# The 16 rows of each stack block are laid seven partitions apart instead of next to each other

## The chip, the cores and the metric

One core of a Trainium2 chip. The metric is the device time of one execution in microseconds (us), the median over several runs. A change counts as faster or slower from 2% on.

## What is computed

Four attention layers on one image of 16 x 16 places with 192 channels (12 heads of 16). Each layer is added to its input after a group norm: `x = x + layer(gn(x))`.

```
layer 0, 3: q,k,v = x@W + b;  a = (q*s)@k.T + rel_h[..., :, None] + rel_w[..., None, :]   # rel = q . table
            out = softmax(a) @ v @ proj + b
layer 1:    layernorm; q,k turned by position; a = q@k.T + bias_head[same or other token]; softmax; @v @wo;
            + residual; layernorm; gelu(x@w1 + b1)@w2 + b2; + residual
layer 2:    keys and values extended by 16 registers; a = q@k_cat.T * s, masked to a 7 x 7 neighbourhood;
            softmax; @v_cat @ out_w.T + b
```

All values are float32.

## The kernel before

Each layer runs in the same stages: group norm, projections to queries, keys and values, filling of two stacks, then for 12 heads the row maxima, scores, exponentials and value products, and the output projection.

**The stacks.** `QS` (two of them, used in turn by layer: layers 0 and 2 the first, 1 and 3 the second) and `KS` hold for each head 128 rows (partitions) over which one matmul contracts. A value is kept as a high and a low part in a short float format, so that the product of a query and a key is three terms, each a block of 16 rows (the head dimension): high times high, low times high, high times low. The blocks lie at partitions 0, 16 and 32 of both stacks. Rows 48 to 63 are zero. Rows 64 to 127 hold four more blocks of 16: the relative position terms of layers 0 and 3 (row high, column high, row low, column low), the token bias of layer 1 or the mask of layer 2; on the key side they hold `hot`, the one-hot rows and columns of each place.

**How they are filled.** SP, the sync engine, issues transfers from SBUF to SBUF. The `move` helper (L307 to L310) waits for the source's signal and issues one transfer to one block; its source is `QH`, `QL`, `KH`, `KL` (96 partitions of 2 KB, two heads each), `QHL` (rows 0 to 63 high, 64 to 127 low parts, in layers 0 and 3), or `RH`, `RL` (row terms in the lower, column terms in the upper 64 partitions). A block is 16 partitions of 12 heads of 256 places, 192 KB. The key stack has 304 places in a head, so its rows are written in pieces of 1 KB. GpSimd issues at the start `hot`, three blocks of zeros and later the mask; it computes layer 1's bias rows itself (L394), from columns that VectorE makes in `bias_cols` (L590 to L599). The registers' keys go into the edges of `KS` by six small transfers of GpSimd (L405).

**Order on TensorE.** After the projections (and `relative`, L849, in layers 0 and 3), `keep_warm(..., DMA_WARM[l])` (L1055) issues 3, 22, 17 or 21 matmuls on `WARM` whose results nobody reads. Then TensorE waits for the stacks (L1056 to L1059). After that `for_maxima` (L870) computes each head's scores for their row maxima, which VectorE reduces (`maximum`, L731, instruction at L738), `turn_early` and `turn_maxima` (L883, L891; instruction at L896) bring the negated maxima into rows, and `scores` (L911) computes the scores again, transposed, with the maxima subtracted by a second matmul. The first `EARLY` = 2 heads are turned by themselves with matmuls that contract over two rows only. Scores are followed by `values` (L926, instruction at L940) after ScalarE's exponential.

In layer 0, VectorE also works off `registers`, `bias_cols` and `reg_selector` (L785 to L787) before its first maximum. After layer 0's last stack transfer SP issues the weights of all later layers (L332, L333).

Of the kernel before, what the change touches and what calls it, by code (L numbers as in the profile page):

```python
# [15 lines left out]
T = SIDE * SIDE  # L49
# [3 lines left out]
HD = 16  # L53
NH = C // HD
HPC = CC // HD
P = 128
# [6 lines left out]
NREG = 16  # L63
# [3 lines left out]
KEY0 = NREG  # L67
REG1 = KEY0 + T
# [8 lines left out]
MASKED = -2.0 ** 100  # L77
LAYERS = 4
REL_LAYERS = (0, 3)

TERMS = ((0, 0), (0, 1), (1, 2))
Q2 = NG * P


VEC = {name: 2 * n for n, name in enumerate(
# [3 lines left out]
SCALED = ("w0", "w2", "w1", "wp", "w3")  # L91

def build(nc, a, out):
    with ExitStack() as ctx:
# [3 lines left out]
        def key_column(l):  # L100

            return Q2 if l in REL_LAYERS else C

        def ps(name, shape):
            return ctx.enter_context(nc.psum_tensor(name, shape, F32))


# [11 lines left out]
        QH = sb("QH", [CC, NC, T], F32R)  # L119
        QL = sb("QL", [CC, NC, T], F32R)  # L120
        KH = sb("KH", [CC, NC, T], F32R)
        KL = sb("KL", [CC, NC, T], F32R)

        QD = sb("QD", [P, NG, T])
        QHL = sb("QHL", [P, NG, T], F32R)
# [6 lines left out]
        RH = sb("RH", [P, NG, T], F32R)  # L132
        RL = sb("RL", [P, NG, T], F32R)
        QS = [sb(f"QS{i}", [P, NH, T], F32R) for i in range(2)]
        KS = sb("KS", [P, NH, KW], F32R)
# [29 lines left out]
        HOT = sb("HOT", [P, T])  # L165
# [5 lines left out]
        ABS = sb("ABS", [P, 3, NH])  # L171
        REGT = sb("REGT", [CC, NC, P])
        KRF = sb("KRF", [CC, NC, NREG])
        KRH = sb("KRH", [CC, NC, NREG], F32R)
        KRL = sb("KRL", [CC, NC, NREG], F32R)
# [6 lines left out]


        RINGS = [[ps(f"RING{r}{i}", [P, 512]) for i in range(2)] for r in range(2)]
# [4 lines left out]
        def hidden(m):  # L189

            return PR[:, m // 2, m % 2 * T:(m % 2 + 1) * T]


# [48 lines left out]
        def slot(*use):  # L242
# [24 lines left out]
                    "qh": {0: NG, 1: 1, 2: NC, 3: NG}, "ql": {0: 1, 1: 1, 2: NC, 3: 1},  # L267
                    "q stack": {0: 2 * 16, 1: 3 * 16, 2: 3 * 16, 3: 2 * 16}}
        signals |= {"kf": {1: 1}}
# [11 lines left out]
        def sem(name):  # L281
            return sems[name]
# [12 lines left out]
        block = ctx.enter_context(nc.Block())  # L295


        @block.sync
        def _(sync):
            def load(wanted):  # L300
                for name, tile, src in wanted:
                    dst = tile[:, :, :] if len(tile.shape) == 3 else tile[:, :]
                    sync.dma_start(dst, a[src]).then_inc(sem(f"{name} loaded"), 16)

            load(loads)
            for l in range(LAYERS):
                def move(signal, stack, src, done, count=None):  # L307

                    sync.wait_ge(*upto(signal, l, count or signals[signal][l]))
                    sync.dma_start(stack.bitcast(F32), src.bitcast(F32)).then_inc(sem(done), 16)  # L310

                queries = QS[l % 2]
                if l in REL_LAYERS:
                    move("qh", queries[32:48, :, :], QHL[0:64, :, :], "q stack")
                else:
                    for row in (0, 32):
                        move("qh", queries[row:row + HD, :, :], QH[:, :, :], "q stack")
                    move("ql", queries[16:32, :, :], QL[:, :, :], "q stack")
                for row in (0, 16):
                    move("kh", KS[row:row + HD, :, KEY0:REG1], KH[:, :, :], "k stack")  # L320
                if l in REL_LAYERS:
                    move("ql", queries[0:32, :, :], QHL[:, :, :], "q stack")
                move("kl", KS[32:48, :, KEY0:REG1], KL[:, :, :], "k stack")
                if l in REL_LAYERS:

                    for w in range(2):
                        for name, row, src in (("rel h", 64, RH), ("rel l", 96, RL)):
                            move(name, queries[row + HD * w:row + HD * w + HD, :, :], src[64 * w:64 * w + 64, :, :],
                                 "rel stack", 2 * w + 2)
                if l == 0:  # L330

                    sync.wait_ge(*upto("rel stack", 0, 64))  # L332
                    load(later_loads)  # L333

            sync.wait_ge(*upto("x", 3, NC))
            sync.dma_start(out, X[:, :, :]).then_inc(sem("stored"), 16)
            sync.wait_ge(sem("stored"), 16)


        @block.gpsimd  # L340
        def _(pool):
            g = nc.gpsimd
# [9 lines left out]
            for col in (slice(0, KEY0), slice(REG1, KW)):  # L352
                g.memset(KS[:, :, col].bitcast(F32), 0.0).then_inc(sem("keys zero"), 1)
            pool.wait_ge(sem("keys zero"), 2)

            pool.dma_start(KS[64:128, :, KEY0:REG1], a["hot"][64:128, None, :].to_broadcast([64, NH, T]))\
                .then_inc(sem("hot rows"), 16)
            for stack in (KS[48:64, :, KEY0:REG1], QS[0][48:64, :, :], QS[1][48:64, :, :]):
                pool.dma_start(stack, a["zeros"]).then_inc(sem("zero rows"), 16)


# [20 lines left out]
            for l in range(LAYERS):  # L382
                if l == 2:

                    pool.wait_ge(*upto("scores", 0, NH))
                    pool.dma_start(QS[0][64:128, :, :], a["mask"][64:128, None, :].to_broadcast([64, NH, T]))\
                        .then_inc(sem("mask rows"), 16)
                if l == 0:


                    pool.wait_ge(sem("ab cols"), 1)
                    loaded(pool, "hot")
                    for h in range(NH):
                        g.tensor_scalar(QS[1][64:128, h, :], HOT[64:128, :], ABS[64:128, 2, h:h + 1],  # L394
                                        ABS[64:128, 1, h:h + 1], ALU.mult, ALU.add).then_inc(sem("ab rows"), 1)
                        pool.wait_ge(sem("ab rows"), h + 1)
                    scale_keys("w1", WQKV[1])
                    scale_keys("wp", WP)
                    scale_keys("w3", WQKV[3], Q2)
                if l == 1:  # L400

                    pool.wait_ge(sem("kr parts"), 2)
                    for col in (0, REG1):
                        for row, src in ((0, KRH), (16, KRH), (32, KRL)):
                            pool.dma_start(KS[row:row + HD, :, col:col + NREG], src[:, :, :])\  # L405
                                .then_inc(sem("kr stack"), 16)


        @block.scalar
        def _(act):  # L410
# [110 lines left out]


            act.preload_act_table_set("natural_log_exp_and_others")
# [36 lines left out]


        @block.vector
        def _(dve):
# [26 lines left out]
            def bias_cols():  # L590

                loaded(dve, "abt", "pcol")
                r = slice(64, 128)
                link(V.tensor_copy(ABH[r], ABT[r]))
                link(V.tensor_tensor(ABL[r], ABT[r], ABH[r].bitcast(F32), ALU.subtract))
                link(V.tensor_scalar(ABS[r, 0:2], ABH[r].bitcast(F32), PCOL[r, 0:1], None, ALU.mult))
                link(V.scalar_tensor_tensor(out=ABS[r, 0:2], in0=ABL[r], scalar=PCOL[r, 1:2], in1=ABS[r, 0:2],
                                            op0=ALU.mult, op1=ALU.add))
                V.tensor_tensor(ABS[r, 2], ABS[r, 0], ABS[r, 1], ALU.subtract).then_inc(sem("ab cols"), 1)  # L599
# [176 lines left out]
            for l in range(LAYERS):  # L776
# [23 lines left out]
                else:  # L800
# [12 lines left out]
                    for i in range(NC):  # L813
                        V.tensor_tensor(X[:, i, :], X[:, i, :], FL[:, i, :], ALU.add).then_inc(sem("x"), 1)


        @block.tensor
        def _(pe):
# [179 lines left out]
            for l in range(LAYERS):  # L998
# [22 lines left out]
                else:  # L1021
                    last = project(lambda m: chunk_psum("q", l, m), WQKV[l], 0, XN, *ready, "q psum" if l == 2 else None)
# [22 lines left out]
                if l == 0:  # L1045
                    registers()
                    pe.wait_ge(sem("hot rows"), 16)
                    pe.wait_ge(sem("zero rows"), 48)
                    pe.wait_ge(sem("backgrounds"), 4)
                if l == 1:  # L1050
                    pe.wait_ge(sem("ab rows"), NH)
                if l == 2:
                    pe.wait_ge(sem("mask rows"), 16)
                    pe.wait_ge(sem("kr stack"), 6 * 16)
# [65 lines left out]


def layouts(inp):
# [3 lines left out]


    order = np.arange(C).reshape(HPC, NC, HD).transpose(1, 2, 0).reshape(C)


# [48 lines left out]
    hot = np.zeros((P, T), f32)  # L1179
    hot[64:80] = hot[96:112] = row == k  # L1180
    hot[80:96] = hot[112:128] = col == k
    first = np.clip(np.arange(SIDE) - 3, 0, SIDE - 7)
    mask = np.zeros((P, T), f32)
    mask[64:80] = np.where((k >= first[row]) & (k < first[row] + 7), 0, MASKED)
    mask[80:96] = np.where((k >= first[col]) & (k < first[col] + 7), 0, MASKED)
    angles = HD // 4
# [6 lines left out]
    pcol = np.zeros((P, 3), f32)  # L1193
    pcol[64:80, 0] = 1
    pcol[96:112, 1] = 1
    pcol[:, 2] = np.arange(P) % 32 < NREG
# [3 lines left out]
    abt = np.zeros((P, 2, NH), f32)  # L1200
    abt[64:128] = L["L1_conv_attn_biases"].T
    regt = np.zeros((CC, NC, GH, 32), f32)
# [14 lines left out]


# [12 lines left out]
```

## Time and profile before

| | |
|---|---|
| Time, median of 3 runs | 290.22 us (287.61 to 291.16) |
| Span of the profiled execution | 287.2 us (the profile gives no other time of it) |
| TensorE busy | 241.8 us (84%), 1255 matmuls; weight loads 149.7 us |
| VectorE busy | 106.3 us (37%) |
| ScalarE busy | 78.7 us (27%) |
| GpSimd busy | 25.3 us (9%) |
| Mean granted TensorE clock | 0.869 of full |
| DMA | 10574 packets, 15.06 MB; 12.63 MB on the queue of SP, 2.24 MB on that of GpSimd |

Busy shares are means over the whole span, in which TensorE's work includes matmuls on `WARM`. A name such as `QS<-QH` is "tile written <- tile read"; buffer numbers are left out. SPq is SP's queue of DMA issues; PE is TensorE, DVE VectorE, ACT ScalarE, POOL GpSimd.

### The profile page before, as it was taken

The page shows a single profiled execution, that of the slowest core. Times are in us where ns is not written, and L with a number is a line of the kernel's source. Part 1 is how long each engine was busy: PE and PEld are TensorE (multiplying, and loading weights), DVE is VectorE, ACT ScalarE, POOL GpSimd, SP SyncE. Part 2 cuts the span into 40 slices and gives each one's busy share as a digit, 9 for nine tenths or more (in the row PEclk, how much of TensorE's full clock was granted, in tenths as well). Part 3 has the DMA queues.
Part 4 walks back from the last instruction along what each step waited for, and adds up shares of the span by engine and source line. Part 5 has one row for each costly group of instructions (what it writes and reads, how often), then busy time and mean ns, then how long its engine had stood idle before and what let it go on. Part 6 is the DMA issues. An engine that isn't in the chain of part 4 may idle for free.

```text
span 287.2 us, 3244 instructions
## 1 busy us (share of the span) xinstructions
PE 241.8 (84%) x1255; PEld 149.7 (52%) x1266; DVE 106.3 (37%) x262; ACT 78.7 (27%) x156; POOL 25.3 (9%) x45
## 2 busy tenths in 40 slices
PE   7856069999899579999989874999999877499995
PEld 2754046555357256655466443665564762375552
DVE  4566034324638133424311522321125651334222
ACT  2581003432030002342252200224321470023431
POOL 7510812601000000000000000000000000000000
PEclk9975557999999955999999996589999977658999
DMA  6999959409003900000000093000000089200000
GB/s 171 236 153 133 123 139 308 69 3 110 2 1 51 113 0 0 2 0 2 0 0 0 3 124 40 0 0 2 0 0 2 27 109 118 21 0 0 0 3 27
DMA packets 10574, 15.06 MB, mean 52 GB/s; under 512 B 2912, under 2 KB 7296, under 8 KB 10528
## 3 DMA queue, kind: packets, MB, share of 16 engines
q1 hardware_dynamic: 7472, 12.63, 28.0%
q0 software_dynamic: 3088, 2.24, 6.3%
q8 instruction: 10, 0.16, 0.3%
q14 instruction: 4, 0.03, 0.0%
HBM read 8.30 MB, written 0.20 MB: 30 GB/s over the span
## 4 chain that ended last, share of the span: by engine, by line
PE 63%; DMA 15%; DVE 7%; ACT 7%; issue 5%; SPq 2%; DVEq 0%; ACTq 0%
PE PC L940 15%; DMA QS<-RL 9%; PE RING L922 8%; PE RING L879 8%; PE RING L923 6%; DMA QS<-QL 4%; PE PB L960 4%; PE RING L824 4%; PE PC L951 2%; DMA RELT<-in_relt 2%; PE PC L865 2%; PE RING L1111 2%; PE PA L1117 2%; PE PC L943 2%; PE PB L824 1%
## 5 line engine op out<-in xcount | busy, mean ns | idle before, releaser
L738 DVE TENSOR_REDUCE NM<-RING 128x2 fp32r<-128x512 f32 (+1 forms) x48 | 30.8, 658 | 73.9 <-PE RING L879 73.5
L879 PE MATMUL RING<-KS,QS 128*128 128x256 f32 (+1 forms) x96 | 28.4, 404 | 28.2 <-DMA QS<-RL 17.4
L824 PE MATMUL RING<-WARM 128*128 128x512 bf16 x195 | 50.0, 401 | 2.3 <-POOL WARM L343 1.3
L940 PE MATMUL PC<-PR,VX 128*32 128x256 f32 x192 | 47.6, 395 | 0.0
L506 ACT ACTIVATE PR<-RING 128x512 f32<-128x512 f32 x48 | 28.6, 595 | 43.0 <-PE RING L923 42.5
L879 PEld LDWEIGHTS RING<-KS,QS 128*128 128x128 f32 x96 | 20.6, 268 | 36.2 <-issue 33.5
L922 PE MATMUL RING<-QS,KS 128*128 128x256 f32 x96 | 34.3, 374 | 0.3
L824 PEld LDWEIGHTS RING<-WARM 128*128 128x128 bf16 x206 | 20.9, 104 | 25.5 <-issue 4.9
L923 PE MATMUL RING<-MT,SELM 128*128 128x256 f32 (+1 forms) x96 | 30.4, 332 | 0.0
L922 PEld LDWEIGHTS RING<-QS,KS 128*128 128x128 f32 x96 | 20.3, 212 | 16.1 <-issue 10.6
L940 PEld LDWEIGHTS PC<-PR,VX 128*32 128x32 f32 x192 | 16.5, 111 | 17.3 <-issue 3.2
L923 PEld LDWEIGHTS RING<-MT,SELM 128*128 128x128 f32 (+1 forms) x96 | 20.4, 213 | 3.3 <-issue 2.7
L494 ACT ACTIVATE MT<-PA 2x256 fp32r<-2x256 f32 x4 | 1.5, 373 | 59.7 <-PE PA L888 59.7
L746 DVE COPY U<-PC 128x256 f32<-128x256 f32 x12 | 5.1, 424 | 27.2 <-PE PC L940 17.4
L751 DVE SCALAR_TENSOR_TENSOR LD<-PC,RD 128x256 f32<-128x256 f32 x12 | 5.1, 425 | 26.4 <-ACT RD L520 26.4
L960 PE MATMUL PB<-O,WO 128*96 128x256 f32 x48 | 12.9, 392 | 0.0
L960 PEld LDWEIGHTS PB<-O,WO 128*96 128x96 f32 x48 | 7.2, 162 | 4.9 <-DVE O L755 1.7
L500 ACT ACTIVATE MT<-PA 128x256 fp32r<-128x256 f32 x12 | 4.6, 382 | 18.6 <-PE PA L896 18.6
L519 ACT ACTIVATE LD<-PC 128x256 f32<-128x256 f32 x12 | 4.6, 386 | 15.3 <-PE PC L951 15.3
L394 POOL TENSOR_SCALAR QS<-HOT,ABS 64x256 fp32r<-64x256 f32 x12 | 6.7, 560 | 14.2 <-DVE ABS L599 13.1
L951 PE MATMUL PC<-U,BSEL 128*128 128x256 f32 x24 | 7.8, 405 | 0.0
L865 PE MATMUL PC<-QC,RELB 128*64 128x48 bf16 x96 | 5.5, 228 | 2.5 <-ACT QC L479 2.5
(153 smaller groups left out, 262.8 us busy)
## 6 DMA issues: line engine op xcount, KB each, us to landing
KS<-KH SPq DMA_DIRECT2D x8, 192.0 KB, 6.8
WQKV<-in_w SPq DMA_DIRECT2D x2, 576.0 KB, 7.2
WO<-in_wo SPq DMA_DIRECT2D x4, 288.0 KB, 9.1
W<-in_ff SPq DMA_DIRECT2D x2, 576.0 KB, 7.6
WQKV<-in_w SPq DMA_DIRECT2D x2, 432.0 KB, 6.6
KS<-in_hot POOLq DMA_DIRECT2D x1, 768.0 KB, 15.4
QS<-QHL SPq DMA_DIRECT2D x2, 384.0 KB, 11.4
KS<-KL SPq DMA_DIRECT2D x4, 192.0 KB, 8.6
```

Source lines behind the costliest of these rows:

```text
L394: g.tensor_scalar(QS[1][64:128, h, :], HOT[64:128, :], ABS[64:128, 2, h:h + 1], ABS[64:128, 1, h:h + 1], ALU.mult, ALU.add).then_inc(sem(" ...
L506: A(PR[:, h % NPR, :], slot("e", l, h)[:, :], ACT.Exp).then_inc(sem("probs"), 1)
L738: V.tensor_reduce(NM[g % 2][:, :, h % GH], slot("m", l, h)[:, 0:2 * n_keys].rearrange("p (q k) -> p q k", q=2), AX.X, ALU.max, negate=True ...
L824: M(bank, WARM[:, 0:P], WARM[:, :], start=True, stop=True)
L865: ins = M(terms.rearrange("p (g c) -> p g c", g=NG), lhsT, q, start=(t == 0), stop=(t == len(TERMS) - 1))
L879: ins = M(s[:, q * n_keys:(q + 1) * n_keys], QS[l % 2][:, h, q * P:(q + 1) * P], KS[:, h, keys], start=True, stop=True)
L922: M(dst, KS[:, h, KEY0 + k * P:KEY0 + (k + 1) * P], QS[l % 2][:, h, :], start=True, stop=False)
L923: ins = M(dst, sel, mt, start=False, stop=True)
L940: ins = M(dst, VX[:, k, h, :], PR[:, h % NPR, k * T:(k + 1) * T], start=(k == 0), stop=(k == 1 and l != 2))
L943: ins = M(dst, VR[:, h, :], PG[g % 2][:, :], start=False, stop=True)
L951: M(PC[g % 2][:, T:2 * T], BSEL[:, :], U[g % 2][:, :], start=True, stop=True)\
L960: ins = M(PB[0:CC, m * T:(m + 1) * T], WO[l][:, g, m * CC:(m + 1) * CC], O[g][:, :], start=(g == 0 and m == 0), stop=(g == NG - 1), skip_g ...
```

## The change

The stacks' rows are dealt out anew. With `BLOCKS = 7` blocks and `FREE = 128 - 7*16 = 16` rows left at the bottom, block b's row k lies at partition 16 + b + 7k. All tensors made outside (`hot`, `mask`, `pcol`, `abt`) follow. What is computed stays the same; a matmul contracts over all 128 rows in any order.

```
+BLOCKS = 7
+FREE = P - BLOCKS * HD
+Q_HIGH, Q_LOW, Q_AGAIN, ROW_HIGH, COL_HIGH, ROW_LOW, COL_LOW = range(BLOCKS)
...
+        def rows_of(stack, block, first=0, last=T):
+            return stack[FREE + block:P:BLOCKS, :, first:last]
...
-                    "q stack": {0: 2 * 16, 1: 3 * 16, 2: 3 * 16, 3: 2 * 16}}
+                    "q stack": {l: 3 * 16 for l in range(LAYERS)}}
...
                 if l in REL_LAYERS:
-                    move("qh", queries[32:48, :, :], QHL[0:64, :, :], "q stack")
+                    for block in (Q_AGAIN, Q_HIGH):
+                        move("qh", rows_of(queries, block), QHL[0:64, :, :], "q stack")
                 else:
-                    for row in (0, 32):
-                        move("qh", queries[row:row + HD, :, :], QH[:, :, :], "q stack")
-                    move("ql", queries[16:32, :, :], QL[:, :, :], "q stack")
-                for row in (0, 16):
-                    move("kh", KS[row:row + HD, :, KEY0:REG1], KH[:, :, :], "k stack")
+                    if l == 1:
+                        sync.wait_ge(sem("ab rows"), NH)
+                    for block in (Q_HIGH, Q_AGAIN):
+                        move("qh", rows_of(queries, block), QH[:, :, :], "q stack")
+                    move("ql", rows_of(queries, Q_LOW), QL[:, :, :], "q stack")
+                for block in (Q_HIGH, Q_LOW):
+                    move("kh", rows_of(KS, block, KEY0, REG1), KH[:, :, :], "k stack")
                 if l in REL_LAYERS:
-                    move("ql", queries[0:32, :, :], QHL[:, :, :], "q stack")
-                move("kl", KS[32:48, :, KEY0:REG1], KL[:, :, :], "k stack")
+                    move("ql", rows_of(queries, Q_LOW), QHL[64:128, :, :], "q stack")
+                move("kl", rows_of(KS, Q_AGAIN, KEY0, REG1), KL[:, :, :], "k stack")
                 if l in REL_LAYERS:
                     for w in range(2):
-                        for name, row, src in (("rel h", 64, RH), ("rel l", 96, RL)):
-                            move(name, queries[row + HD * w:row + HD * w + HD, :, :], src[64 * w:64 * w + 64, :, :],
-                                 "rel stack", 2 * w + 2)
+                        for name, block, src in (("rel h", ROW_HIGH, RH), ("rel l", ROW_LOW, RL)):
+                            move(name, rows_of(queries, block + w), src[64 * w:64 * w + 64, :, :], "rel stack", 2 * w + 2)
...
-            pool.dma_start(KS[64:128, :, KEY0:REG1], a["hot"][64:128, None, :].to_broadcast([64, NH, T]))\
-                .then_inc(sem("hot rows"), 16)
-            for stack in (KS[48:64, :, KEY0:REG1], QS[0][48:64, :, :], QS[1][48:64, :, :]):
+            for block in (ROW_HIGH, COL_HIGH, ROW_LOW, COL_LOW):
+                pool.dma_start(rows_of(KS, block, KEY0, REG1),
+                               a["hot"][FREE + block:P:BLOCKS, None, :].to_broadcast([HD, NH, T])).then_inc(sem("hot rows"), 16)
+            for stack in (KS[0:FREE, :, KEY0:REG1], QS[0][0:FREE, :, :]):
                 pool.dma_start(stack, a["zeros"]).then_inc(sem("zero rows"), 16)
...
-                        g.tensor_scalar(QS[1][64:128, h, :], HOT[64:128, :], ABS[64:128, 2, h:h + 1],
-                                        ABS[64:128, 1, h:h + 1], ALU.mult, ALU.add).then_inc(sem("ab rows"), 1)
+                        g.tensor_scalar(QS[1][:, h, :], HOT[:, :], ABS[:, 2, h:h + 1], ABS[:, 1, h:h + 1], ALU.mult, ALU.add).then_inc(sem("ab rows"), 1)
...
-                r = slice(64, 128)
+                r = slice(0, P)
...
```

The mask of layer 2 and `hot` are each written by four transfers of one block instead of one of 64 partitions, and the registers' keys go to the same blocks. GpSimd's bias rows now fill all 128 rows of layer 1's query stack (the other blocks with zeros, since their columns are zero), and this is why SP waits for them (`ab rows`) before it writes the queries of layer 1, and why the zeros of the second query stack are no longer transferred. In layers 0 and 3 the high parts of the queries go out twice by a transfer each; before, the second copy went with the low parts in one transfer to 32 rows. The counts on which TensorE waits follow.

## Rows read from the trace of the kernel before

**Rows 1.** The page, 40 slices of 7.18 us: granted TensorE clock in tenths, and GB/s.

```profile
PEclk9975557999999955999999996589999977658999
GB/s 171 236 153 133 123 139 308 69 3 110 2 1 51 113 0 0 2 0 2 0 0 0 3 124 40 0 0 2 0 0 2 27 109 118 21 0 0 0 3 27
```

**Rows 2.** TensorE in order of time: start us, length us, work [idle before it <-releaser].

```profile
38.71 1.19 PE L879 MATMUL RING<-KS,QS 128*128 128x256 f32 x4 [12.17 <-DMA QS<-RL]
...
92.27 4.91 PE L824 MATMUL RING<-WARM 128*128 128x512 bf16 x21
102.12 1.19 PE L879 MATMUL RING<-KS,QS 128*128 128x256 f32 x4 [4.93 <-issue]
...
166.77 3.83 PE L824 MATMUL RING<-WARM 128*128 128x512 bf16 x16
176.45 1.14 PE L879 MATMUL RING<-KS,QS 128*128 128x192 f32 x4 [5.85 <-issue]
...
236.27 6.25 PE L824 MATMUL RING<-WARM 128*128 128x512 bf16 x20 [0.33 <-issue]
247.79 1.19 PE L879 MATMUL RING<-KS,QS 128*128 128x256 f32 x4 [5.26 <-DMA QS<-RL]
```

**Rows 3.** SP's queue in order of time: start us and length us of an issue.

```profile
23.96 0.60 SPq L310 DMA_DIRECT2D QS<-RL  x1
...
93.25 1.26 SPq L310 DMA_DIRECT2D KS<-KH  x2
94.55 0.62 SPq L310 DMA_DIRECT2D KS<-KL  x1
...
164.44 1.32 SPq L310 DMA_DIRECT2D QS<-QH  x2
...
167.76 0.62 SPq L310 DMA_DIRECT2D KS<-KL  x1
...
237.08 0.59 SPq L310 DMA_DIRECT2D QS<-RL  x1
```

**Rows 4.** DMA issues near 23.96, 90.00, 94.55, 167.76, 237.08 us; KB, us to landing.

```profile
QS<-RL SPq DMA_DIRECT2D x1, 192.0 KB, 14.5
...
QS<-QH SPq DMA_DIRECT2D x1, 192.0 KB, 3.9
...
KS<-KL SPq DMA_DIRECT2D x1, 192.0 KB, 7.5
...
KS<-KL SPq DMA_DIRECT2D x1, 192.0 KB, 8.6
...
QS<-RL SPq DMA_DIRECT2D x1, 192.0 KB, 10.5
```

**Rows 5.** Stretches of 2 us: TensorE busy (instructions), clock, DMA busy share, GB/s.

```profile
42.00:44.00 2.00, 2.00 (x9) 1.00 1.03 281
...
92.00:94.00 2.00, 1.95 (x10) 1.00 1.06 120
...
96.00:98.00 2.00, 1.19 (x6) 1.00 1.15 114
...
106.00:108.00 2.00, 2.00 (x6) 0.50 0.00 0
...
166.00:168.00 2.00, 2.00 (x12) 1.00 1.06 157
```

**Rows 6.** VectorE in order of time, layer 0, columns as in rows 2.

```profile
28.35 0.20 DVE L580 COPY SELR<-IDF 128x64 f32<-128x64 f32 x1
39.52 1.29 DVE L738 TENSOR_REDUCE NM<-RING 128x2 fp32r<-128x512 f32 x2 [10.97 <-PE RING L879]
```

**Rows 7.** TensorE in order of time: the second turn of maxima, layers 0, 1, 3.

```profile
49.59 0.34 PE L896 MATMUL PA<-IDR,NM 128*128 128x128 f32 x2
...
114.85 0.34 PE L896 MATMUL PA<-IDR,NM 128*128 128x128 f32 x2
...
261.07 0.34 PE L896 MATMUL PA<-IDR,NM 128*128 128x128 f32 x2
```

More of the change, by code:

```diff
@@ L385, in _ @@
                     pool.wait_ge(*upto("scores", 0, NH))
-                    pool.dma_start(QS[0][64:128, :, :], a["mask"][64:128, None, :].to_broadcast([64, NH, T]))\
-                        .then_inc(sem("mask rows"), 16)
+                    for block in (ROW_HIGH, COL_HIGH, ROW_LOW, COL_LOW):
+                        pool.dma_start(rows_of(QS[0], block), a["mask"][FREE + block:P:BLOCKS, None, :].to_broadcast([HD, NH, T]))\
+                            .then_inc(sem("mask rows"), 16)
                 if l == 0:
@@ L403, in _ @@
                     for col in (0, REG1):
-                        for row, src in ((0, KRH), (16, KRH), (32, KRL)):
-                            pool.dma_start(KS[row:row + HD, :, col:col + NREG], src[:, :, :])\
+                        for block, src in ((Q_HIGH, KRH), (Q_LOW, KRH), (Q_AGAIN, KRL)):
+                            pool.dma_start(rows_of(KS, block, col, col + NREG), src[:, :, :])\
                                 .then_inc(sem("kr stack"), 16)
@@ L1046, in _ @@
                     registers()
-                    pe.wait_ge(sem("hot rows"), 16)
-                    pe.wait_ge(sem("zero rows"), 48)
+                    pe.wait_ge(sem("hot rows"), 4 * 16)
+                    pe.wait_ge(sem("zero rows"), 2 * 16)
                     pe.wait_ge(sem("backgrounds"), 4)
@@ L1052, in _ @@
                 if l == 2:
-                    pe.wait_ge(sem("mask rows"), 16)
+                    pe.wait_ge(sem("mask rows"), 4 * 16)
                     pe.wait_ge(sem("kr stack"), 6 * 16)
@@ L1179, in layouts @@
     hot = np.zeros((P, T), f32)
-    hot[64:80] = hot[96:112] = row == k
-    hot[80:96] = hot[112:128] = col == k
+    block = [slice(FREE + b, P, BLOCKS) for b in range(BLOCKS)]
+    hot[block[ROW_HIGH]] = hot[block[ROW_LOW]] = row == k
+    hot[block[COL_HIGH]] = hot[block[COL_LOW]] = col == k
     first = np.clip(np.arange(SIDE) - 3, 0, SIDE - 7)
     mask = np.zeros((P, T), f32)
-    mask[64:80] = np.where((k >= first[row]) & (k < first[row] + 7), 0, MASKED)
-    mask[80:96] = np.where((k >= first[col]) & (k < first[col] + 7), 0, MASKED)
+    mask[block[ROW_HIGH]] = np.where((k >= first[row]) & (k < first[row] + 7), 0, MASKED)
+    mask[block[COL_HIGH]] = np.where((k >= first[col]) & (k < first[col] + 7), 0, MASKED)
     angles = HD // 4
@@ L1193, in layouts @@
     pcol = np.zeros((P, 3), f32)
-    pcol[64:80, 0] = 1
-    pcol[96:112, 1] = 1
+    pcol[block[ROW_HIGH], 0] = 1
+    pcol[block[ROW_LOW], 1] = 1
     pcol[:, 2] = np.arange(P) % 32 < NREG
@@ L1200, in layouts @@
     abt = np.zeros((P, 2, NH), f32)
-    abt[64:128] = L["L1_conv_attn_biases"].T
+    abt[:] = L["L1_conv_attn_biases"].T
     regt = np.zeros((CC, NC, GH, 32), f32)
```

## Prediction

> **What bounds the kernel now.** I read the page's slices first: four valleys in TensorE's granted clock (slices 4 to 6, 15 and 16, 25 and 26, 33 to 36, counted from 1), each in or right behind slices in which DMA moves about 110 to 150 GB/s, while one slice of weight loads moves 308 [rows 1]. These are the four layers' hand-overs: the projections are done, the stacks QS and KS are being filled, and no score can be computed. TensorE in order of time [rows 2] gives the four waits: the first `for_maxima` starts at 38.71, 102.12, 176.45 and 247.79, after 12.17, 4.93, 5.85 and 5.26 us of idle time, together 28.2; warm-up matmuls end at 97.18, 170.60 and 242.52 in layers 1 to 3 (start plus length). The view calls two of them "issue", but the transfers explain them: the last one issued before each wait [rows 3] lands so long after its issue [rows 4]: 23.96 + 14.5 = 38.5, 94.55 + 7.5 = 102.05, 167.76 + 8.6 = 176.4, 237.08 + 10.5 = 247.6. Each is within 0.25 us of TensorE's start. So the waits are transfers and nothing else.
>
> **Why these transfers are slow.** In layers 1 and 2 six transfers of 192 KB (1.18 MB) are in flight and move 114 to 120 GB/s with all DMA engines shown busy [rows 5]. The queries (runs of 2 KB, a source row) go at 120 at 92 to 94 us, the keys (runs of 1 KB, since a head of KS is wider than its 256 places) at 114 at 96 to 98; a price per packet would have made the two differ. The fastest such stretch is 166 to 168 us with 157 GB/s [rows 5]: there a write to partitions 16 to 31 (QL) is in flight beside one to 32 to 47. That speaks for a limit on the place of the destination: 16 neighbouring partitions share few ways in. Weight loads, written to 96 or 128 partitions, go at 281 GB/s on the same queue [rows 5].
>
> The Trainium skill, "SBUF — State Buffer", section "Door 1: The DMA port swizzle", has this as a rule: a partition's bits 4 to 2 and 6 choose one of 16 ports, partitions 0 to 15 reach 4 ports and measured 104 GB/s, all 128 reach 16 and measured 328. The trace's 114 and 281 agree. By that map each block of the change (16 + b + 7k) reaches 14 or 15 ports, with at most two rows on one.
>
> **The change, part by part.**
> The stack transfers keep their count of bytes, runs and source order; only their 16 destination rows spread over 106 partitions. Rate afterwards: no row shows SBUF to SBUF at a spread destination. Bounds: 157 (that fastest stretch) and 308 GB/s (loads). I take 250, nearer the loads, since the spread is like theirs, but 64 source partitions (QHL, RH, RL) may narrow the reading. A transfer's latency beside its data: the first QS<-QH of layer 1, alone in the queue, landed after 3.9 us [rows 4]; 197 thousand bytes at 115 GB/s is 1.7, leaving 2.2, of which about half lies before the data. At 250 a lone transfer would land after 2.2 + 0.8 = 3.0.
>
> Layer 1: keys are issued from 93.25 to 94.55 [rows 3]; the queries (0.59 MB from about 91.1) are gone by 93.5 at 250. Keys' data: 94.3 + 590/250 = 96.7, plus 1.1 = 97.8. The warm-up matmuls end at 97.18, so they cap the gain at 4.93; I take 102.1 − 97.8 = 4.3. At 157: data until about 98.6, landing at 99.7, gain 2.4.
> Layer 2: all six are issued within 3.3 us from 164.44. 165.5 + 1180/250 + 1.1 = 171.3, gain 5.1; cap 5.85 (cover until 170.60); at 157: 174.1, gain 2.3.
> Layer 3: the last is issued at 237.08, and at 250 GB/s little is queued before it (1.97 MB in all from 228.7 on, 7.9 us): it lands near 240.1, 2.4 us under the cover of the 20 warm-up matmuls that end at 242.52. Gain 5.26, the whole wait. At 157 the data take 12.5 us, until 241.2, plus 1.1: 242.3, just covered.
> Layer 0: to 14.4 us (2 slices of 7.18 at 171 and 236 GB/s, 2.92 MB) loads run freely. Slices 3 to 5 move 153, 133 and 123 [rows 1]: 2.94 MB. The change takes 0.2 MB of it away (zeros of the second query stack, now written by GpSimd). 2.74 MB at 250 are done at 25.4; the last issue at 23.96 lands at 27.0. At 157: 31.9 + 1.1 = 33.0. What is late next is VectorE: its work for the registers and the layer 1 bias ends at 28.55, and the first maximum started at 39.52 [rows 6]. So it can start 10.9 earlier; at 157 GB/s 5.7.
> Waits together: 10.9 + 4.3 + 5.1 + 5.3 = 25.6; at 157: 5.7 + 2.4 + 2.3 + 5.3 = 15.7; caps: 10.9 + 4.93 + 5.85 + 5.26 = 26.9.
>
> The clock. After the waits of layers 1 to 3 the granted clock lies at 0.5 (1.2 GHz) into the twelfth microsecond: at 106 to 108 it is 0.50 though TensorE is never idle there, after 1.00 up to the wait [rows 5]. From the first `for_maxima` to the turn of the second set of maxima (L896) takes 114.85 − 102.12 = 12.73 in layer 1 and 261.07 − 247.79 = 13.28 in layer 3, but 49.59 − 38.71 = 10.88 in layer 0 [rows 2, 7], where the clock was back at 1.00 from 42 to 44 [rows 5]. With a wait of 0 to 0.7 us the clock has no idle stretch to fall in, and I take layer 0's length for layers 1 and 2, gains of 1.9 each, and 13.28 − 10.88 = 2.4 for layer 3. Layer 2's stretch has register matmuls between, but its clock is low as long. Layer 0 goes the other way: it starts while the clock is down, in another phase of it; priced with layer 1's length it loses 12.73 − 10.88 = 1.9. Sum: 1.9 + 1.9 + 2.4 − 1.9 = 4.3. Bounds: 0 and 9 (a stretch never slowed, estimated at 9.5 us from layer 0's, less 3.2 us at half clock at its start and 2.7 us later, in all four layers).
>
> The Trainium skill, "TensorE: Matmul & The Clock Gate", section "HAM oscillation — how this bites in real kernels", says that waits for DMA put the clock down each time and that the next work starts cold. The rows at 106 to 108 us agree.
>
> Edits that cost nothing. One more SP issue in layers 0 and 3 (QHL's high half twice instead of 32 rows at once), 0.6 us [rows 3]: it goes out with the first signal, while SP waits for the keys' signal behind it; uncovered it would be those 0.6. GpSimd issues 6 transfers instead of 4 at the start, at about the same length 1.2 us more, before it scales w0's keys; the query projection runs meanwhile on TensorE, and without that cover it would cost up to 1.2. Four mask transfers for one go out after layer 0's scores, a whole layer before their use. The 12 `tensor_scalar` of L394 and five of `bias_cols` work on 128 partitions for 64 with the same number of elements in each, and so at equal length; layer 1 reads their result 50 us later. SP's new wait on "ab rows" is met long before layer 1; the query and key transfers are queued behind it, but their own signals come later. The later weight loads start 11 us sooner and land long before layer 1.
>
> **The sum.** 25.6 + 4.3 = 29.9; the span of 287.2 becomes 257.3. The profiled execution's span is 3.0 under the median of the three runs (290.22, from 287.61 to 291.16; the profile gives no total of its own), so 290.2 − 29.9 = 260.3; if its own time was that of the fastest run, 257.7. I predict 260.
>
> **Rivals.**
> A. The spread helps, but only to some 157 GB/s: several engines still meet on one way in, or 64 source partitions bind. Gains 15.7, and with leftover waits of 2 to 4 us half of the clock's part: 18, time 272. For it: the only mixed SBUF to SBUF stretch. Against it: its two groups of 16 were still packed.
> B. Each transfer is limited by the engines' handling, not by the destination's place. Nothing changes, one more issue: 290. For it: no transfer between SBUF tensors is seen above 157. Against it: equal rates for runs of 1 and 2 KB, and the jump to 157 with two groups.
> C. On the other side: rows that aren't neighbours are cut into more or worse distributed pieces, so that a transfer runs on half the engines' rate. Deciding point: a rate under 114 GB/s. At 57 the 1.18 MB of layers 1 and 2 take 10.3 us more each, layers 0 and 3 about as much or more: slower by over 40, 330. Against it: each row of a stack is 12 KB by itself before and after, and nothing can be merged across partitions in either.
> D. Waits go, but the clock stays down: the maxima phase with its two-row matmuls lets it fall by itself, as it did in layer 0 between 44 and 48 us even without idle time. 25.6 alone, 264.6; with layer 0 losing 2, 266. For it: that second fall.
>
> **How the numbers follow.** Forecast 0.60 (253 to 264), D 0.16, A 0.13, B 0.06, C 0.03, and 0.02 for more than forecast, down to 250. A range from 253 to 270 takes the forecast, D and a part of A, whose other part, B, C and the low end are left out: about 0.8. About 2% (5.8 us) is what a measurement of this kernel tells from no change. Faster by over 2%: forecast, D, A and the low end: 0.91; within 2%: B, 0.06; slower: C, 0.03.
>
> **What would show it.** Per step: last landings 3 to 4 us after issue instead of 7.5 to 14.5; DMA at 200 to 300 GB/s in the hand-overs; TensorE's first `for_maxima` within 1 us of its warm-up matmuls in layers 1 to 3; the first maximum of layer 0 at 28.6; clock 1.00 across the hand-overs and stretches of 10 to 11 us to L896. I would be wrong if landings stayed at 7 us or more (B), or if the stretches kept 12.7 (D).

## The result

The median fell from 289.22 us (4 runs, 287.61 to 291.16) to 259.13 us (4 runs, 256.18 to 260.93): 30.1 us or 10%. Executions of a program fall into a faster and a slower state, and the ratio of 0.8878 (95% interval 0.8817 to 0.8938), 11% less, compares fast ones alone, which for the changed kernel are those of 257.62 and 256.18 us. The profiled executions have spans of 287.2 and 255.5 us, 31.7 apart. The forecast of 260, faster, held.

The page of the changed kernel: TensorE's granted clock in tenths, and GB/s, in 40 slices, now of 6.39 us; and the two DMA queues with packets, MB and their share of 16 engines' span.

```profile
PEclk9995555999999999999999999899999997979999
GB/s 153 259 195 188 169 275 218 14 0 122 1 4 0 125 60 0 3 0 3 0 0 0 0 50 138 0 0 3 0 0 3 0 103 191 16 0 0 1 3 31
...
q1 hardware_dynamic: 7504, 12.63, 20.7%
q0 software_dynamic: 3152, 2.04, 5.1%
```

Three of the four valleys of [rows 1] have nearly closed; the first is as deep as it was. SP's queue moved the same 12.63 MB in 20.7% of a shorter span instead of 28.0%: its packets stood in the engines for less time.

TensorE in order of time, with the waits that answer to [rows 2] and the second turn of maxima (L859, L896 before) that answers to [rows 7]:

```profile
29.66 1.20 PE L842 MATMUL RING<-KS,QS 128*128 128x256 f32 x4 [5.24 <-DMA QS<-RL]
43.44 0.52 PE L859 MATMUL PA<-IDR,NM 128*128 128x128 f32 x2
...
86.35 4.91 PE L787 MATMUL RING<-WARM 128*128 128x512 bf16 x22
91.74 0.72 PE L842 MATMUL RING<-KS,QS 128*128 128x256 f32 x4 [0.48 <-issue]
100.80 0.34 PE L859 MATMUL PA<-IDR,NM 128*128 128x128 f32 x2
...
152.74 3.83 PE L787 MATMUL RING<-WARM 128*128 128x512 bf16 x17
157.43 0.66 PE L842 MATMUL RING<-KS,QS 128*128 128x192 f32 x4 [0.85 <-issue]
169.09 0.35 PE L859 MATMUL PA<-IDR,NM 128*128 128x128 f32 x2
...
214.01 5.14 PE L787 MATMUL RING<-WARM 128*128 128x512 bf16 x21
218.81 0.83 PE L842 MATMUL RING<-KS,QS 128*128 128x256 f32 x4
229.38 0.34 PE L859 MATMUL PA<-IDR,NM 128*128 128x128 f32 x2
```

The waits went from 12.17, 4.93, 5.85 and 5.26 us to 5.24, 0.48, 0.85 and none. In layer 3 `for_maxima` stands right behind the warm-up matmuls, as forecast.

The last transfers before these points, issues at 23.91, 88.62, 154.22 and 215.23 us, with KB and us to landing (answers to [rows 4]: 14.5, 7.5, 8.6, 10.5):

```profile
QS<-RL SPq DMA_DIRECT2D x1, 192.0 KB, 5.5
...
KS<-KL SPq DMA_DIRECT2D x1, 192.0 KB, 3.0
...
KS<-KL SPq DMA_DIRECT2D x1, 192.0 KB, 3.1
...
QS<-RL SPq DMA_DIRECT2D x1, 192.0 KB, 3.1
```

Stretches of 2 us, columns as in [rows 5] (TensorE busy, clock, DMA share, GB/s): layer 0 first, then the hand-overs of layers 1 and 2.

```profile
16.00:18.00 2.00, 0.83 (x26) 1.00 1.54 110
18.00:20.00 2.00, 2.00 (x53) 1.00 1.15 121
20.00:22.00 2.00, 0.96 (x8) 0.59 1.01 141
22.00:24.00 2.00, 2.00 (x7) 0.50 1.10 221
24.00:26.00 2.00, 0.41 (x1) 0.50 1.11 249
...
86.00:88.00 2.00, 2.00 (x12) 1.00 0.71 214
...
96.00:98.00 2.00, 2.00 (x12) 1.00 0.00 0
...
154.00:156.00 2.00, 2.00 (x11) 1.00 0.95 276
```

Layer 2's burst of six transfers goes at up to 276 GB/s where it went at 114 to 157, and at 96 to 98 us, two microseconds into layer 1's scores, the clock is 1.00. (A second profile of the same kernel, the "same again" of the last table, has 0.60 at 94 to 96 us and 0.54 at 96 to 98, in the same work.) But in layer 0 the rate is 110 to 141 GB/s from 16 to 22 us, as if nothing had been spread; only then does it rise.

**Where 31.7 us came from.** Each is a difference of two rows, start against start. Waits (end of the work before, or landing, to the first `for_maxima`): 38.71 − 29.66 = 9.05 in layer 0 (TensorE's own idle time fell by 6.93, since the work before it ended 2.1 us sooner, which counts for nothing while the landing comes last); in layer 1 the gain up to `for_maxima` is 102.12 − 91.74 = 10.38, of which 92.27 − 86.35 = 5.92 was there before its warm-up, so 4.46; in layer 2 likewise 19.02 − 14.03 = 4.99; in layer 3 28.98 − 22.26 = 6.72, of which 5.26 is the wait and 1.46 a faster warm-up at a higher clock. Waits together: 23.8. From first `for_maxima` to the second turn: 10.88 became 13.78 in layer 0 (−2.90), 12.73 became 9.06 in layer 1 (+3.67), 14.46 became 11.66 in layer 2 (+2.80, with the turn at 190.91 in the profile of before), 13.28 became 10.57 in layer 3 (+2.71). With the 1.46 the clock's part is 7.7. The rest is 0.2. The second profile of the changed kernel gives the clock 5.5 by the same differences: −0.01, +2.44, +1.65 and +1.45, and nothing from layer 3's warm-up.

### The profile page after: what moved, and what is told of

It is laid out like the page before. It is cut to its first block, busy times and chain, and to the rows that moved or that the text cites. A ratio compares the mean times of both kernels' runs of the same rounds, so it can differ in the third digit from the quotient of the medians.

```text
span 255.5 us, 3263 instructions
## 1 busy us (share of the span) xinstructions
PE 232.7 (91%) x1266; PEld 142.0 (56%) x1266; DVE 105.8 (41%) x262; ACT 78.6 (31%) x156; POOL 27.1 (11%) x50
## 3 DMA queue, kind: packets, MB, share of 16 engines
q1 hardware_dynamic: 7504, 12.63, 20.7%
## 4 chain that ended last, share of the span: by engine, by line
PE 73%; DVE 8%; ACT 7%; SPq 4%; DMA 4%; issue 2%; DVEq 0%; ACTq 0%
PE PC L903 17%; PE RING L787 9%; PE RING L885 9%; PE RING L886 6%; PE RING L842 6%; PE PB L923 5%; SPq L277 3%; PE PC L914 2%; DMA QS<-RL 2%; PE RING L1074 2%; PE PA L1080 2%; PE PC L806 2%; PE PC L906 2%; DMA RELT<-in_relt 2%; PE PA L806 1%
## 5 line engine op out<-in xcount | busy, mean ns | idle before, releaser
L787 PE MATMUL RING<-WARM 128*128 128x512 bf16 x206 | 51.9, 400 | 1.3 <-POOL WARM L311 1.3
L885 PE MATMUL RING<-QS,KS 128*128 128x256 f32 x96 | 32.7, 358 | 1.4 <-ACT MT L460 0.8
L842 PE MATMUL RING<-KS,QS 128*128 128x256 f32 (+1 forms) x96 | 23.5, 345 | 6.8 <-DMA QS<-RL 5.2
L886 PE MATMUL RING<-MT,SELM 128*128 128x256 f32 (+1 forms) x96 | 28.6, 315 | 0.0
L885 PEld LDWEIGHTS RING<-QS,KS 128*128 128x128 f32 x96 | 19.5, 203 | 16.4 <-issue 10.4
L903 PEld LDWEIGHTS PC<-PR,VX 128*32 128x32 f32 x192 | 16.5, 111 | 17.1 <-issue 2.9
L842 PEld LDWEIGHTS RING<-KS,QS 128*128 128x128 f32 x96 | 16.7, 223 | 14.4 <-issue 10.7
L886 PEld LDWEIGHTS RING<-MT,SELM 128*128 128x128 f32 (+1 forms) x96 | 19.5, 203 | 2.5 <-issue 0.9
L923 PE MATMUL PB<-O,WO 128*96 128x256 f32 x48 | 12.9, 392 | 0.0
L362 POOL TENSOR_SCALAR QS<-HOT,ABS 128x256 fp32r<-128x256 f32 x12 | 6.7, 554 | 13.1 <-DVE ABS L563 12.0
L396 ACT ACTIVATE GT<-GT 96x2 f32<-96x2 f32 x4 | 0.8, 203 | 22.1 <-DVE GT L585 22.1
```

The lines of the kernel that those rows point to most:

```text
L362: g.tensor_scalar(QS[1][:, h, :], HOT[:, :], ABS[:, 2, h:h + 1], ABS[:, 1, h:h + 1], ALU.mult, ALU.add).then_inc(sem("ab rows"), 1)
L787: M(bank, WARM[:, 0:P], WARM[:, :], start=True, stop=True)
L842: ins = M(s[:, q * n_keys:(q + 1) * n_keys], QS[l % 2][:, h, q * P:(q + 1) * P], KS[:, h, keys], start=True, stop=True)
L885: M(dst, KS[:, h, KEY0 + k * P:KEY0 + (k + 1) * P], QS[l % 2][:, h, :], start=True, stop=False)
L886: ins = M(dst, sel, mt, start=False, stop=True)
L903: ins = M(dst, VX[:, k, h, :], PR[:, h % NPR, k * T:(k + 1) * T], start=(k == 0), stop=(k == 1 and l != 2))
```

## The experiments

Three questions: is it the place of the destination rows and nothing else in the change; what about the place counts; and how much is the clock, in particular why layer 0 gained less of the wait than forecast and lost on its clock. The runs came in three sets, with medians of "before" of 290.7, 289.7 and 290.1 us.

**Packed: the new kernel with its rows side by side.**

```
-            return stack[FREE + block:P:BLOCKS, :, first:last]
+            return stack[block_rows(block), :, first:last]
+def block_rows(b):
+    return slice(16 * ((b + 1) % 8), 16 * ((b + 1) % 8) + 16)
```

(The tensors made outside follow, and the zero rows are a block too, in this and the next three.)

> The changed kernel with its rows put next to each other again (block b at partitions 16(b+1) to 16(b+1)+15); the doubled query copy, the split hot and mask transfers and the one zero transfer less stay. Theory (the place of the destination rows makes it all): the waits of layers 1 to 3 are back at 4 to 6 us, the last transfers land 7 to 11 us after issue, 114 to 120 GB/s; layer 0's first for_maxima near 37 (0.2 MB less). Time 284 to 291. Rival (the other edits help): waits under 3 us, time under 275.

290.92 us median, ratio to before 1.0017 (0.9974 to 1.0060). The last transfers landed 14.6, 7.5, 8.3 and 10.4 us after issue, TensorE waited 11.64, 4.99, 5.90 and 5.17 us. Everything that the layout gave is gone, and the other edits (a second copy of the high parts, four transfers in place of one, one block of zeros less) are together worth nothing measurable. The first `for_maxima` of layer 0 came at 39.3 us, where 37 was expected for the 0.2 MB less.

**Strides of 2, 4 and 8.**

```
stride 2:   return slice(32 * (b // 2) + b % 2, 32 * (b // 2) + 32, 2)
stride 4:   return slice(64 * (b // 4) + b % 4, 64 * (b // 4) + 64, 4)
stride 8:   return slice(b, P, 8)
```

> Rows of a block two partitions apart, so a block lies within 32 partitions. Theory of the map of ways in (Door 1, a span of 32 reaches twice as many as one of 16): about twice 115, 200 to 230 GB/s; last key transfer of layer 2 lands 3.5 to 5 us after issue (3.1 at stride 7, 8.6 packed). Rival (distance between rows counts, each neighbour hurts): rates near 120 to 160, landing 6 us or more. Time by the theory 258 to 266, by the rival 272 to 285.

> Rows of a block eight partitions apart over all 128 partitions. By the map of ways in, they reach only 8 of 16, as at stride 2, so the same rates and landings as at stride 2 (layer 2's last key transfer 3.5 to 5 us, time 258 to 266). Rival (the wider the spread, the faster): as at stride 7 or better, 3.1 us or less, time 255 to 261.

> Rows of a block four partitions apart, within 64 partitions. By the map of ways in this is again 8 of 16, so landings as at strides 2 and 8 (last key transfer of layer 2 4.0 to 4.6 us, of layer 1 3.5); if the span of partitions counted, it would lie between stride 2 and 7 and under 3.4 in layer 1. Time 257 to 264.

| rows of a block | partitions spanned | last key transfer, layer 1 / layer 2, us to landing | waits in layers 1, 2, 3, us | time, us |
|---|---|---|---|---|
| side by side | 16 | 7.5 / 8.3 | 4.99, 5.90, 5.17 | 290.92 (10 runs) |
| 2 apart | 31 | 3.5 / 4.5 | 1.00, 1.73, 0.99 | 260.66 (2 runs), ratio 0.8985 (0.8885 to 0.9085) |
| 4 apart | 61 | 3.5 / 4.4 | 0.92, 1.93, 0.60 | 261.03 (1 run) |
| 8 apart | 121 | 3.5 / 4.1 | 0.89, 1.64, 0.90 | 260.71 (2 runs), ratio 0.8986 (0.8858 to 0.9115) |
| 7 apart | 106 | 3.0 / 3.1 | 0.48, 0.85, 0 | 259.13 (4 runs), ratio 0.8878 (0.8817 to 0.8938) |

Layer 2's burst, the stretches in which its rate is highest and those after it, stride 2, then stride 8, then stride 7's last (columns as above):

```profile
152.00:154.00 2.00, 2.00 (x11) 1.00 1.00 234
154.00:156.00 2.00, 1.95 (x10) 1.00 1.15 190
```

```profile
154.00:156.00 2.00, 1.95 (x11) 1.00 0.96 260
156.00:158.00 2.00, 1.86 (x9) 1.00 1.12 198
```

```profile
156.00:158.00 2.00, 1.15 (x8) 1.00 0.24 75
```

Distance doesn't order the rows of the table: 8 apart spans more than 7 apart and lands later, and 2, 4 and 8 apart land alike within 0.4 us though they span 31, 61 and 121 partitions. While data is queued they settle at 190 to 198 GB/s, 1.7 times the packed 114 and a little under the 200 to 230 expected. The stride of 7 shows no such queue: it lands near the price of a lone transfer. A map of ways in puts them in this order: 4 for the packed block, 8 for strides of 2, 4 and 8, and 14 or 15 for 7; an order of spans does not. The map is that of the Trainium skill, "SBUF — State Buffer", section "Door 1: The DMA port swizzle", from whose rule these counts are worked out. The page measured 189 and 196 GB/s for the 8 ports of spans of 32 and 64 partitions; the 190 to 198 of the runs agree. In time the four layouts differ by less than these few runs can tell: one or two microseconds of wait.

**The kernel before, kept warm.**

```
-DMA_WARM = (3, 22, 17, 21)
+DMA_WARM = (47, 44, 43, 44)
```

> The kernel before with 47, 44, 43 and 44 warm-up matmuls at the hand-overs in place of 3, 22, 17 and 21, so that TensorE is busy until the stacks land. Transfers unchanged. Theory (about a quarter of the gain, 7 to 8 us, is the clock that no longer falls): time 289 less 6 to 11, 278 to 283, for_maxima still starting at the landings, stretches to L896 of 9 to 11 us. Rival (the clock's part is nothing or is paid by the waits alone): 286 to 291.

281.75 us median, ratio 0.9717 (0.9635 to 0.9798): 8 to 9 us off 290.7, with the transfers as slow as ever (landings of 16.5, 6.2, 8.8 and 10.4 us). So a share of the cost of a slow transfer was never its wait but the clock that fell in it. The stretches to the second turn were 11.1, 11.8, 11.7 and 10.4 us where they had been 10.9, 12.7, 14.5 and 13.3. Layers 0 and 1 did not reach the 9 us that layer 1 has in the changed kernel: the clock fell to 0.50 at 40 us in layer 0, behind a gap of 2.3 us, and at 108 us in layer 1, almost five microseconds after `for_maxima` began, with TensorE busy for 1.80 and 1.73 of each 2 us just before. In layer 1 the two-row matmuls lie there (from 106.57 us).

**Zero rows by GpSimd.** In layer 0's stretch of 110 to 141 GB/s two transfers are in flight that still write 16 neighbouring partitions. GpSimd issues them; the next rows are from the changed kernel's GpSimd in order of time and its DMA issues (us to landing last).

```profile
5.63 0.57 POOL L328 DMA_DIRECT2D KS<-in_zeros  x1
6.16 0.55 POOL L328 DMA_DIRECT2D QS<-in_zeros  x1
```

```profile
KS<-in_zeros POOLq DMA_DIRECT2D x1, 192.0 KB, 13.5
QS<-in_zeros POOLq DMA_DIRECT2D x1, 192.0 KB, 16.6
```

They land at 19.1 and 22.8 us, and at 22 us the rate rises. This kernel takes them away:

```
-            for stack in (KS[0:FREE, :, KEY0:REG1], QS[0][0:FREE, :, :]):
-                pool.dma_start(stack, a["zeros"]).then_inc(sem("zero rows"), 16)
...   (after the loop of "backgrounds")
+            for stack in (KS[0:FREE, :, KEY0:REG1], QS[0][0:FREE, :, :]):
+                g.memset(stack.bitcast(F32), 0.0).then_inc(sem("zero rows"), 1)
```

> The changed kernel with its two blocks of zero rows (partitions 0 to 15 of the key stack and of the first query stack) written by GpSimd, after its other fills, instead of by two transfers. Theory: these two, the only large transfers left that write to 16 neighbouring partitions, hold all engines between 16 and 22 us in layer 0 (110 to 141 GB/s there), so without them that stretch goes at 200 GB/s or more, the last transfer of layer 0 lands at 27 us or before instead of 29.4 and the first for_maxima starts 2.4 to 3.5 us earlier; time 255 to 258 against 259. Rival (it is the sum of bytes and the loads from HBM): 0.4 MB less gives at most 1.6 us and the stretch stays under 160 GB/s.

260.47 us median, ratio 0.8937 (0.8861 to 0.9013): no gain, and a miss for both theories. GpSimd, then VectorE, in order of time:

```profile
10.91 2.65 POOL L347 MEMSET KS<- 16x3072 f32 x1
13.51 2.79 POOL L347 MEMSET QS<- 16x3072 f32 x1
```

```profile
11.14 2.57 DVE L665 CAST QB<-QD 128x256 bf16<-128x256 f32 x1
13.63 2.82 DVE L666 CAST QHL<-QD 128x256 fp32r<-128x256 f32 x1
```

Two casts of VectorE that take 0.28 to 0.29 us in the changed kernel take 2.57 and 2.82, each ending 0.15 us after a GpSimd fill. They feed everything in layer 0, so the stack transfers are issued some 5 us later and this run can't answer the question. The Trainium skill, "SBUF — State Buffer", section "Who interferes with whom", says that a VectorE cast in its two-port form and a GpSimd instruction exclude each other for the whole instruction; the lengths of these rows agree, though no row shows in which form the casts ran.

Three runs above do answer it. At strides of 2, 4 and 8 the zero rows are a block that is dealt out like the others, with the same bytes and the same loads. Stride 2, columns as in [rows 5] but with GpSimd's busy time in place of TensorE's:

```profile
16.00:18.00 2.00, 0.00 (x0) 1.00 1.52 231
18.00:20.00 2.00, 0.00 (x0) 1.00 1.03 211
20.00:22.00 2.00, 0.00 (x0) 1.00 1.14 198
```

Stride 4 has 233, 205 and 195 GB/s in these stretches and stride 8 has 227, 194 and 194, where the changed kernel has 110, 121 and 141 (92, 138 and 198 in its second profile). Their last transfer of layer 0 lands at 27.8 to 28.7 us against 29.4, though their other blocks are spread less well. So it is the place of the zero rows that holds the rate down, and not their bytes or the loads.

**No zero rows at all.** Blocks from partition 0 on, and matmuls over 112 rows:

```
-FREE = P - BLOCKS * HD
+USED = BLOCKS * HD
-            return stack[FREE + block:P:BLOCKS, :, first:last]
+            return stack[block:USED:BLOCKS, :, first:last]
-                    ins = M(..., QS[l % 2][:, h, q * P:(q + 1) * P], KS[:, h, keys], ...)
+                    ins = M(..., QS[l % 2][0:USED, h, q * P:(q + 1) * P], KS[0:USED, h, keys], ...)
```

(and so in `reg_scores` and `scores`; both zero transfers and the wait for them are gone)

> The changed kernel with the blocks at partitions b + 7k from 0 on and matmuls that contract over partitions 0 to 111, so that no zero rows are needed: no transfer is left that writes to 16 neighbouring partitions, and nothing takes their place on another engine. Theory (the two zero transfers clog layer 0's queues, and in the kernel with GpSimd fills only the blocked casts of VectorE hid it): 16 to 22 us goes at 200 GB/s or more, VectorE's casts stay at 0.29 us, the last stack transfer of layer 0 lands at 26 to 27.5 us, first for_maxima 2 to 3.5 us earlier than 29.7. Time 1 to 4 us under the changed kernel of the same call. Rival (loads and bytes bound layer 0): at most 1.6 us earlier, 16 to 22 us under 160 GB/s.

258.94 us median against 258.35 for the changed kernel in the same set of runs, so no gain that can be told where 1 to 4 us were expected. In the trace the theory holds in the main: the transfers run freely, the last one lands at 25.7 us and VectorE's casts of these values stay at 0.29 us but one of 0.59. TensorE, then VectorE, in order of time:

```profile
24.87 1.49 PE L785 MATMUL RING<-WARM 128*128 128x512 bf16 x3
25.99 1.22 PE L840 MATMUL RING<-KS,QS 112*128 112x256 f32 x4
...
40.38 0.34 PE L857 MATMUL PA<-IDR,NM 128*128 128x128 f32 x2
```

```profile
28.05 0.19 DVE L542 COPY SELR<-IDF 128x64 f32<-128x64 f32 x1
28.15 1.28 DVE L700 TENSOR_REDUCE NM<-RING 128x2 fp32r<-128x512 f32 x2
```

TensorE has no wait left before layer 0's `for_maxima`. Data moves at 244 GB/s from 14 to 16 us and at 170 to 239 from 16 to 22, with the DMA engines' share down to 0.65 to 0.87 and landings 2.8 to 4.3 us after issue, so the queue runs empty between issues; `for_maxima` starts at 25.99 instead of 29.79. What is late next is VectorE, at 28.15, just behind its own preparation, as forecast for the change itself. But the second turn is at 40.38, against 40.68 in the changed kernel's profile of the same set: the stretch is 14.4 us, nearly all of it at a clock of 0.50 (it is back only between 38 and 40 us), where the other had 10.9. Of the 3.8 us, 3.5 were given back to the clock.

**Warm-up matmuls for the gaps that are left.**

```
after_warm:     DMA_WARM = (19, 24, 20, 21)
zeros_warm:     DMA_WARM = (10, 24, 20, 21), zero rows by GpSimd
rows112_warm:   DMA_WARM = (12, 24, 20, 21), 112 rows
```

> The changed kernel with 19, 24, 20 and 21 warm-up matmuls instead of 3, 22, 17 and 21, which fills the remaining gaps of TensorE (5.2, 0.5, 0.85 and 0 us). Theory (in layer 0 the clock stays down because TensorE idles until the landing; 13.8 us from first for_maxima to the second turn there against 9.1 in layer 1): the clock is up at the landing and the stretch is 9 to 11.5 us, time 255 to 257. Rival (the maxima phase pulls it down by itself): the stretch stays over 12.5, time as the changed kernel's, 258 to 260.

> Both edits, with 10 warm-up matmuls in layer 0 for the shorter wait. Both theories: for_maxima of layer 0 near 26.8 and a stretch of 10 to 12 us: time 252 to 255. If the two aren't additive (warm-up at half clock fills only the shorter gap and the clock isn't up yet): 255 to 257.

> The same with 12, 24, 20 and 21 warm-up matmuls. Theory: layer 0's for_maxima starts where the landing or the 12 warm-up matmuls end (26.5 to 28 us), with the clock up sooner: stretch to the second turn 10.5 to 12.5 us; 2 to 4 us under the changed kernel with its own warm-up counts. Rival (in layer 0 the clock falls by itself): no difference from 112 rows alone.

> The changed kernel as it is, in the same call, so that the others are compared on one chip: 256 to 261.

| | median, us (4 runs each) | `for_maxima` of layer 0 | to the second turn, layers 0 to 3 |
|---|---|---|---|
| changed kernel | 259.13 (256.18 to 260.93) | 29.66 | 13.8, 9.1, 11.7, 10.6 |
| the same again | 258.35 (257.52 to 259.70) | 29.79 | 10.9, 10.3, 12.8, 11.8 |
| its gaps filled | 256.97 (255.48 to 258.63) | 30.34 | 11.8, 10.6, 12.9, 10.7 |
| zero rows by GpSimd | 260.47 (258.23 to 261.50) | 30.82 | 14.5, 10.6, 12.9, 10.7 |
| the same, gaps filled | 260.17 (258.74 to 261.65) | 33.08 | 10.6, 10.4, 12.8, 10.7 |
| 112 rows | 258.94 (257.56 to 260.30) | 25.99 | 14.4, 11.2, 11.6, 11.8 |
| 112 rows, gaps filled | 257.74 (255.40 to 258.69) | 28.76 | 10.6, 11.2, 11.6, 11.8 |

The "same again" and the two kernels with 112 rows are one set of runs, the three between them another, and the first line stands by itself. The first two lines are one and the same program, and its stretches differ by up to 2.9 us in a layer. The ratio of the changed kernel with filled gaps is 0.8843 (0.8776 to 0.8911), that of the changed kernel 0.8878 (0.8817 to 0.8938): the intervals overlap, so it may be 1 us faster and isn't shown to be. Its layer 0 stretch, 11.8 us, lies between the bounds of theory and rival, and decides nothing, since the kernel with its gaps unfilled has 10.9 in one of its two profiles. With 10 or 12 warm-up matmuls before a landing that needs fewer, the stretch is 10.6 in place of 14.4, but the start is up to 2.8 us later. The clock can be bought with idle TensorE time, at nearly its price. Both kernels missed their forecasts: 260.17 us against 252 to 257, with `for_maxima` at 33.08 and not near 26.8, and 0.6 us under the changed kernel of its set against 2 to 4.

## Why the prediction was right, and where it was off

**The bound and the cause** held: the hand-overs were transfers into packed rows. Packed again, all of it came back; the rest of the change together counts for nothing measurable. The evidence read from before (equal rates for runs of 1 and 2 KB, 157 GB/s where two groups of 16 were written at once) pointed to the right limit, and rival B (engines' handling) is out. Rivals A (no faster than 157) and C (slower in pieces) are out with it.

**The rate** of 250 was a choice between 157 and 308: measured 214 to 276 in bursts. In layer 2 the six transfers hardly queued: they landed 2.9 to 3.2 us after issue, the last at 154.22 + 3.1. A lone transfer was put at 3.0 us; those of layers 1 and 2 took 2.6 to 3.2. The 3.9 us from which the 3.0 was worked out wasn't of a lone transfer either: the row of SP's queue has two `QS<-QH`, the second about 0.6 us behind the first.

**The waits**, layer by layer (forecast, measured): 10.9, 9.05; 4.3, 4.46; 5.1, 4.99; 5.26, 5.26. Sum 25.6 against 23.8. The miss is layer 0. There the step was "2.74 MB at 250 are done at 25.4, the last issue lands at 27.0"; it took the stretch from 14.4 us on as a whole at the new rate. Two transfers in it were not spread, the zero rows, which the change itself puts at partitions 0 to 15, and while they were in flight the whole queue went at 110 to 141 GB/s, the spread transfers included; the last one landed at 29.4. With the zero rows dealt out too (strides of 2, 4 and 8) the same stretch went at 194 to 233, and without them (112 rows) `for_maxima` started at 25.99. I had counted their bytes and not their place. "What is late next is VectorE, at 28.55" was right, at 28.15, but only in that kernel.

**The clock** was mis-sized: 4.3 forecast, 7.7 in this profile and 5.5 in the second one of the same kernel. Layers 1 and 2 were priced with layer 0's 10.88 us, a stretch that begins at half clock and falls once more; layer 1 was 9.06, and 10.29 in the second profile. Layer 0 was forecast to lose 1.9; it lost 2.9 here and nothing in the second profile (10.89 against 10.88), so that its sign came true was luck. Layer 3's warm-up matmuls also ran faster by 1.46, which had no term, and did not in the second profile. The bound of 9 doesn't come out of its working: 3.2 and 2.7 us at half clock are 3.0 lost at most, which leaves 7.9 of layer 0's 10.88 and not 9.5, and with 9.5 the layers 0, 1 and 3 alone give 8.4. The forecast's errors, 3.4 too little here and 1.8 too much in the waits, have opposite signs, which is part of why 260 was met.

**Rival D** (the waits go, the clock stays down by itself) was wrong as a whole and has a true core: the clock does fall behind the landing with TensorE at work, in the kernel before kept warm (layer 1) and in the changed kernel itself, where it is 0.50 at 164 to 166 us in layer 2 and at 226 to 228 in layer 3. What makes it fall there wasn't tested by itself; the two-row matmuls of `EARLY` are the suspects by place only, and the same matmuls ran at 1.00 throughout in layer 1 of the changed kernel's first profile.

**The cover** held everywhere: the extra issue of SP, two more of GpSimd, the bias rows on 128 partitions. SP's new wait on `ab rows` was met at 34 us, 50 us before it was asked for.

## What to carry to other kernels

Where many transfers write one block of 16 neighbouring partitions, compare GB/s in that stretch with the loads' and, if it is a fraction, deal the rows out; any stride brought most of it, and the odd one, 7, landed soonest. Then look for the transfers that were left packed, since one of them in the queue slows all the others. Count a wait of TensorE at more than its length: here 24 us of waits carried 5.5 to 8 us of lost clock with them, by the profile, and removing layer 0's last wait bought nothing, because the clock took it. And don't read a clock effect of 3 us in one stretch from one profile: the same program showed both values.

## What the runs showed of the hardware that I had not expected

- Transfers that are spread go no faster than a packed one as long as it shares the engines with them: 110 to 141 GB/s from 16 to 22 us, 221 in the 2 us in which it landed, and 194 to 233 from 16 to 22 us where it was spread too.
- GpSimd fills of 16 x 3072 values (2.65 and 2.79 us) held up VectorE's casts one for one: 2.57 and 2.82 us instead of 0.29.
- The same program has stretches of 13.8 or 10.9 us for the same matmuls, by the moment at which its clock comes up (still 0.50 at 42 to 44 us, or 1.00 at 34 to 36); five further kernels that moved layer 0's start by 0.7 to 3.7 us ended within 2.2 us of the changed kernel.
